# Attention and mixture of experts on one core: value products two steps behind the scores, five exp buffers, one row of maxima

## What is computed

```python
    q_mag = jax.nn.softplus(q)
    k_mag = jax.nn.softplus(k)
    ...
    scores = jnp.einsum('bhsd,bhtd->bhst', q_embed, k_embed) / D ** 0.5
    attn = jax.nn.softmax(scores, axis=-1)
    out = jnp.einsum('bhst,bhtd->bhsd', attn, v)
    ...
x = _layernorm(x + _L0_attn_ref(...), axis=-1)
x = _layernorm(x + _L0_ffn_ref(...), axis=-1)
```

## Time and profile before

| | |
|---|---|
| median of 3 runs | 917.41 us (916.76 to 917.43) |
| the profiled execution | 918.83 us, span 917.0 us |
| busy in the span | PE 878.5, ACT 736.7, DVE 635.7, PEld 498.4, POOL 481.5 us |
| mean granted clock of PE | 0.986 of full |

### The profile page before, as it was taken

One profiled execution on the slowest core, in us unless ns is written; L12 is line 12 of the kernel. 1 busy time (PEld: TensorE's weight loads), 2 busy tenths in 40 slices (PEclk: granted clock), 3 DMA queues, 4 the chain that ended last, 5 costly groups with the idle time before them and its releaser, 6 DMA issues. The chain is left out here.

```text
span 917.0 us, 20105 instructions
## 1 busy us (share of the span) xinstructions
PE 878.5 (96%) x7673; PEld 498.4 (54%) x7673; DVE 635.7 (69%) x1177; ACT 736.7 (80%) x911; POOL 481.5 (53%) x408
## 2 busy tenths in 40 slices
PE   7999999999999999999999999999399999999995
PEld 5434344433344434334443433333299999999995
DVE  5788556547886645799565577527657887888786
ACT  5698978897897899889789889898355787778875
POOL 3388245245575635657563454441512556666574
PEclk9999999999999999999999999999789999999998
DMA  5644456643535345263433525612170745534411
GB/s 176 161 131 140 145 211 222 226 168 106 185 128 213 119 131 208 87 206 135 165 110 111 195 87 182 205 54 84 60 244 32 242 151 185 172 115 134 157 63 64
DMA packets 62508, 135.47 MB, mean 148 GB/s; under 512 B 10558, under 2 KB 31398, under 8 KB 62272
## 3 DMA queue, kind: packets, MB, share of 16 engines
q1 hardware_dynamic: 41648, 72.61, 24.4%
q0 software_dynamic: 20464, 61.18, 19.0%
q10 hardware_dynamic: 288, 0.27, 0.1%
HBM read 69.20 MB, written 62.35 MB: 143 GB/s over the span
## 5 line engine op out<-in xcount | busy, mean ns | idle before, releaser
L814 ACT ACTIVATE prob<-spsum 128x1024 f32<-128x1024 f32 x512 | 492.7, 1022 | 83.0 <-PE spsum L1036 79.2
L1060 PE MATMUL opsum<-prob,val 128*17 128x512 f32 x2048 | 270.1, 597 | 3.9 <-ACT prob L814 1.9
L1036 PE MATMUL spsum<-stacks 32*128 32x512 f32 x1536 | 135.5, 426 | 2.0 <-issue 1.3
L1036 PEld LDWEIGHTS spsum<-stacks 32*128 32x128 f32 x1536 | 73.5, 183 | 117.0 <-ACT prob L814 65.8
L1036 PEld LDWEIGHTS spsum<-area_q 32*128 32x128 f32 x1536 | 73.1, 183 | 112.7 <-ACT prob L814 57.1
L1036 PE MATMUL spsum<-area_q 32*128 32x512 f32 x1536 | 132.7, 425 | 1.1 <-ACT prob L814 1.1
L1452 DVE RECIPROCAL oden<-oden 128x256 f32<-128x256 f32 x62 | 108.7, 1753 | 2.1
L608 POOL TENSOR_TENSOR area_s<-emb,area_s 128x1024 fp32r<-128x1024 f32 x28 | 66.7, 2380 | 48.4 <-DVE area_s L1259 45.0
L694 POOL TENSOR_TENSOR onorm<-oraw,oden 128x512 f32<-128x512 f32 x31 | 42.1, 1358 | 93.3 <-DVE oden L1452 93.2
L1060 PEld LDWEIGHTS opsum<-prob,val 128*17 128x17 f32 x2048 | 39.4, 95 | 84.9 <-ACT prob L814 46.2
L606 POOL TENSOR_TENSOR square<-raw 128x512 bf16<-128x512 f32 x28 | 52.5, 1877 | 56.4 <-DVE raw L1232 56.3
(11 more groups left out here) (278 smaller groups left out, 1375.8 us busy)
## 6 DMA issues: line engine op xcount, KB each, us to landing
split_scratch<-area_s POOLq DMA_DIRECT2D x56, 512.0 KB
area_k<-in_w SPq DMA_DIRECT2D x16, 1024.0 KB, 6.9
area_q<-split_scratch SPq DMA_DIRECT2D x28, 512.0 KB
stacks<-split_scratch SPq DMA_DIRECT2D x24, 512.0 KB
rows<-dispatched SPq DMA_DIRECT2D x7, 662.5 KB
aT<-onorm SPq DMA_DIRECT2D x124, 32.0 KB
staged<-in_xT SPq DMA_DIRECT2D x7, 512.0 KB, 4.2
dispatched<-last_rows POOLq DMA_DIRECT2D x2, 1722.5 KB, 13.1
```

The source lines that it names most:

```text
L814: act.activation(prob[u % NPB][:], spsum[u % NSB][:].rearrange("p a n -> p (a n)"), ACT.Exp, scale=HD ** -0.5).then_inc(s_exp, 1)
L1036: ins = pe.matmul(spsum[u % NSB][:, j % 2, :], kst[par][rows, a, P * kt:P * (kt + 1)], qst[par][rows, b, cols], start=i == 0, stop=i == 2 ...
L1060: ins = pe.matmul(opsum[32 * j:32 * j + HD + 1, :], val[b % 2][:, kt, h0 + j, :], prob[(2 * s + j // 2) % NPB][:, HALF * (j % 2):HALF * (j ...
```

## The change

- The ring of exp buffers has five instead of four (`NPB = 5`). The condition of exp(u) keeps its form, so its number changes.
- `values(s - 2)` stands after `scores(s)` and the jobs of step s, where `values(s - 1)` stood. The last two steps' values come after the last scores.
- `read_outputs` stands at the head of step 8k+1 instead of 8k.
- One `row_max` instead of two; the last group uses `x_lo` instead. This is in the form with maxima only.

```diff
-        row_maxs = [sb(f"row_max{i}", [P, SEQ], F32R) for i in range(2)]
+        row_max = sb("row_max", [P, SEQ], F32R)
+
+        def row_max_of(grp):
+
+            return x_lo[:, 0] if grp == NG - 1 else row_max
...
-        NPB, NSB = 4, 3
+        NPB, NSB = 5, 3
...
                 if shifted:
-                    if grp:
-                        values(s0 - 1)
+                    for s in range(max(s0 - 2, 0), s0):
+                        values(s)
...
                     for job in jobs_at(s):
                         run(job)
-                    if s > s0 or s and not shifted:
-                        values(s - 1)
+                    if s >= s0 + 2 or s >= 2 and not shifted:
+                        values(s - 2)
...
                 if s == NSTEP:
+                    values(s - 2)
                     last_tokens(TB // 2)
                     values(s - 1)
...
-                if 0 < s < NSTEP and s % TB == 0:
+                if 1 < s < NSTEP and s % TB == 1:
                     read_outputs(s // TB - 1)
```

More of the change, by code:

```diff
@@ L476, in add_maxima @@
                     for j in range(GH):
-                        sp.dma_start(row_maxs[grp % 2][ROWS * j:ROWS * j + 1].bitcast(F32),
+                        sp.dma_start(row_max_of(grp)[ROWS * j:ROWS * j + 1].bitcast(F32),
                                      grow[TB * j:TB * (j + 1)].bitcast(F32)).then_inc(g_row, 16)
@@ L1044, in scores @@
                         ins = pe.matmul(spsum[u % NSB][:, j % 2, :], row_ones[ROWS * j:ROWS * j + 1],
-                                        row_maxs[par][ROWS * j:ROWS * j + 1, cols], start=False, stop=True)
+                                        row_max_of(grp)[ROWS * j:ROWS * j + 1, cols], start=False, stop=True)
                         if j % 2 == 1:
```

## The result

| | before | changed |
|---|---|---|
| median | 917.42 us (916.76 to 918.63, 4 runs) | 959.19 us (957.39 to 962.79, 4 runs) |
| profiled execution, span | 918.83, 917.0 | 958.53, 956.7 |

The changed kernel takes 1.0451 times the time of before, with an interval of 1.0422 to 1.0480: 41.8 us more. The forecast was 33 more, 950, with a range of 935 to 962.

The account below looks back on a forecast made before the run. Three score tiles were taken to bound quiet steps, PE steps with a job. Terms 26.4 + 1.5 + 4.2 + 1.5 - 3.7 + 2.0 + 1.3 = 33.2 put the median at 950 us, range 935 to 962.

Parts of the forecast that it names:

- the fourth rival: Whole kernel: waits meet, late values on DVE hold back POOL and the next job, 1.5 not 0.7; 958 to 975, chance 0.09.
- The main term: Steps with a softplus: exp(2s+1) waits for values behind the job, softplus loses its cover; 22 units x 1.2 = 26.4 us.
- The quiet steps: Some 150 steps without a job: 0.02 won and 0.03 lost by turns, taken as 0, bounds -2 and +3 us.
- Collisions: Steps 41, 42, 49, 50 of three batches: job reading behind the later copy on DVE delays next job, 6 x 0.7 = 4.2.
- Late copies: Five block ends where values waited for DVE's late copy: now wanted a step later, -3.7 us, bounds -6 and 0.
- Step 246: Its job waits for gathered heads, whose chain starts with a copy now a step later: PE waits 2.0 us, bounds 0 and 2.1.
- Cast and functions: ACT's cast L822 and functions L787, L788 lose cover behind pinned exps: 1.5 us in all, bounds 0 and 3.
- Start and tail: Jobs at 249 and 250, values moved behind the last scores and away from step 2: +1.3 us, bounds -1 and 3.
- The signs: What would show it: late exp(2s+1), no idle by softplus, 22 to 28 longer places only there, PE idle up some 30 us.
- The lag pays: Rival: exp buffer or values' wait makes the 0.2 us of every second quiet step; -15, 902 us, chance 0.04.
- Half of it: Rival: PE's later scores give ACT's delay back, 0.6 a softplus, or DVE gains more; 919 to 938, chance 0.13.
- More of it: Rival: waits meet through DVE, and ACT's delays recur in the steps after; 958 to 975, chance 0.09.

## Why the prediction was right, and where it wasn't

- **The number.** 959.2 lies in the stated range, 935 to 962, but 1.2 outside the forecast's own band of 938 to 958, on the side of the fourth rival. The terms left out partly cancelled: 7.6 more at steps without a term and 2.6 at steps 90 and 154, against 3.3 less at eight places. That the range held owes something to this luck; that the time rose, and why, doesn't.
- **The main term** held in mechanism and size: 22 x 1.2 = 26.4 against 26.3 measured, and two edits that leave the rest as it is take it away, one by moving the softplus, one by a sixth buffer. Its parts erred in both directions. The wait behind the values is 0.13, not 0.04, so a place costs 1.25 (18 of them lie between 1.18 and 1.29), and four cost less, three of these because they were late before already (step 15: 2.86 before, 0.49 more; steps 112 and 176: 2.3 before, 1.0 more).
- **All other steps, taken as 0: measured 7.6.** This is the largest term that was mis-sized; the forecast and the spans are 33 and 40 apart from the kernel before. The quiet steps themselves were right: the 123 of them without a job hold 2.1, within the bounds of -2 to +3. The other 5.5 are in steps with a job, for which the sum had no term: the new wait costs 0.1 in most `qk` steps. Nor is the delay of a softplus over after two steps, where the prediction has "the pattern goes on as before": at step 64 the second exp starts late again, for the next values, and step 66 takes 0.47 more, 36 0.52, 184 0.40 and some fifteen others 0.2 to 0.3. That it is nearly all the same wait is shown: with six buffers these are at 0.1 to 0.2, all but step 233 (0.4).
- **Latency.** I took 0.04 from the end of the values to the exp; the rows above have 189.28 to 189.41. That makes exp(2s+1) start 2.08 after the scores instead of 1.99, exp(2s+2) 1.12 instead of 1.00.
- **Collisions**: 0.7 each was right, the seventh (250) was counted in the tail. The experiment that puts the reading first takes all seven away.
- **Late copies**: -3.7 was right for the five places it was read from, -3.5. But I took the copy at 89 as in time one step later, and did not look at what DVE does in that step. It does the routing chain of step 88, and the copy moved behind it: +1.3 each at 90 and 154. Steps 82 and 146 pay for the move of the copy too, 0.4 here and 2.4 to 6.4 where no softplus wait covers it.
- **Step 246**: 2.0 forecast, 1.7 measured. **Cast and functions**: 1.5, measured 1.9. **Start and tail**: +1.3 forecast with step 250 (0.7), measured -0.5 without it; it would be some +0.6 to +0.9 but for the long start of the profiled execution of the kernel before (1.1 to 1.4).
- **The signs.** The exp behind its own step's values, the missing idle time behind the softplus, and the 22 places came out. "No such place elsewhere" did not: 90 and 154 take 1.3 longer and 246 1.7, for DVE's sake. PE's idle time went from 38.5 us of the span to 63.2, 25 more and not 30.
- **Rivals.** "The lag pays" is out, and by the run with six buffers too, where the wait is gone and the lag gives nothing: the exps of quiet steps stay at the pace that three score tiles set. "Half of it" would have needed PE to give the delay back. It does so only behind the softplus of step 75, where 1.4 of 1.7 come back at 79, 143 and 207; of the 26.3 it gives back nothing that the steps show. "More of it" (958 to 975) had the measured time just inside it, and one of its two reasons happened: the delays recur in the steps after. The other did not: the collisions stayed at 0.7.

## What to carry to other kernels

Ring depth and lag are one quantity: what counts is where in the reader's order the work stands that frees a buffer, seen from the writer that needs it. One more buffer and one more step of lag left an exp waiting for work of its own step, behind the job, and 1.2 us of softplus in the in-order queue behind that exp lost its cover 22 times; moving the softplus in front of the waiting exp bought back 25.6 us, a sixth buffer all 32.

Before adding a lag, ask which gap it would close. Here the gap was a score tile, and with every buffer wait away the second step of lag still cost 0.75%, through the copy at each block's end: a wait moved by one step on an engine is queued behind other work there, and that step has to be read too.

## What the runs showed of the hardware

- An exp that waits for the values starts 0.13 us after their end (189.28 to 189.41 above; the median of 163 such waits in the changed kernel, and of 214 in the kernel with three buffers); one that waits for its scores starts 0.045 after them (median of 155 in the kernel before; both by the ends that the profile models for PE). Each exp has two waits, and the one for the values is held by an instruction of its own on ACT's sequencer. In the changed kernel, between 189 and 190 us (count, duration in ns, first and last start):

```profile
L817 ACTq EVENT_SEMAPHORE  x1: 17/17/17, 189.3 to 189.3; - x1
```

It starts some 0.06 after the values' end, and the exp some 0.06 after it. In the kernel before, the instruction of the same kind (L813) lies ahead of the exp by 0.9 us in the median, and the exp waits for its scores. By these rows the 0.09 is the way through that instruction; no run took it away. The Trainium skill ("Perfetto Trace Analysis", "Identifying Dependency Chains") says that an instruction with waits on several engines may have such a one in front; it gives no time for it. Here both waits are for PE.
- DVE's product of 128 x 1024 (`emb`) takes 1.22 us in nearly all cases, and 3.29 in the row at step 82 above. All ten traces together have 320 of these products. 29 of them ran beside a product on POOL that reads two tiles (`x_lo`, `wqk_lo`, `wv_lo`, `onorm`), and all 29 took 1.53 to 3.33; of the other 291 only two took more than 1.23 (1.53 both), though 237 ran beside POOL's squaring of one tile. At step 82, POOL:

```profile
224.10 2.83 POOL L644 TENSOR_TENSOR x_lo<-staged,aT 128x1024 fp32r<-128x1024 f32 x1
```

  No run took POOL's product away, so that it is the cause is likely but not shown.
